# Identities multiplied into a free bank during two waits of TensorE, and experts copied on chip instead of gathered

## What is computed

```python
h = jnp.square(jax.nn.relu(jnp.einsum('bsd,fd->bsf', x, W_fc)))
y = jnp.einsum('bsf,df->bsd', h, W_proj)
def step(mem, _):
    reset = jax.lax.stop_gradient(spike_fn(mem - THRESHOLD))
    mem_new = BETA * mem + y - reset * THRESHOLD
    spk = spike_fn(mem_new - THRESHOLD)
    return (mem_new, spk)
_, spks = jax.lax.scan(step, mem0, None, length=NUM_STEPS)
return jnp.sum(spks, axis=0) / NUM_STEPS
```

```python
ffn_probs = jax.nn.softmax(jnp.mean(n2, axis=1) @ ffn_rw + ffn_rb, axis=-1)
topk_p, topk_i = jax.lax.top_k(ffn_probs, K)
topk_p = topk_p / jnp.sum(topk_p, axis=-1, keepdims=True)
sw1 = fw1[topk_i]
sw2 = fw2[topk_i]
h = jax.nn.gelu(jnp.einsum('btd,bkdf->bktf', n2, sw1), approximate=False)
eo = jnp.einsum('bktf,bkfd->bktd', h, sw2)
return x + jnp.einsum('bktd,bk->btd', eo, topk_p)
```

## Time and profile before

| what | value |
| --- | --- |
| runs | 2107.44, 2114.57, 2112.74 us; median 2112.74 |
| profiled execution | 2107.44 us, span 2105.7 us |
| TensorE busy | 1726.3 us, 82% of the span |
| VectorE busy | 1291.6 us, 61% |
| ScalarE busy | 1169.0 us, 56% |
| GpSimd busy | 611.3 us, 29% |
| mean granted clock of TensorE | 0.904 of full speed |

### The profile page before, as it was taken

How to read it: one execution, slowest core, us unless ns; L and a number is a source line. 1 busy time by engine, 2 the same in 40 slices (tenths; PEclk the granted TensorE clock), 3 DMA queues, 4 the chain that set the end, 5 groups by cost and what they waited for, 6 DMA issues and landing times.

```text
span 2105.7 us, 36738 instructions
## 1 busy us (share of the span) xinstructions
PE 1726.3 (82%) x13696; PEld 902.9 (43%) x13696; DVE 1291.6 (61%) x2587; ACT 1169.0 (56%) x2722; POOL 611.3 (29%) x759
## 2 busy tenths in 40 slices
PE   5997889798898979889588885968999676899976
PEld 1555345533355425543244332323554352355435
DVE  4775478545776467745477267636878445678844
ACT  3565355543465536565256554554888635388862
POOL 2552155300544035410255103313332031333202
PEclk9999999999899989999679696986999988699997
DMA  4000000000000000000252000005443020544303
GB/s 174 17 17 7 0 16 17 12 0 1 16 12 17 1 11 17 17 1 0 45 99 50 1 1 0 0 18 110 89 97 74 2 80 8 111 97 94 76 2 100
DMA packets 55272, 79.21 MB, mean 38 GB/s; under 512 B 6004, under 2 KB 38996, under 8 KB 54584
## 3 DMA queue, kind: packets, MB, share of 16 engines
q1 hardware_dynamic: 52536, 68.47, 14.8%
q0 software_dynamic: 2560, 8.39, 1.3%
HBM read 50.59 MB, written 16.88 MB: 32 GB/s over the span
## 4 chain that ended last, share of the span: by engine, by line
PE 58%; DVE 16%; ACT 13%; issue 7%; DMA 3%; POOL 3%; SPq 0%; DVEq 0%; POOLq 0%; ACTq 0%
PE ps L195 53%; ACT arena L583 4%; DVE arena L1331 2%; PE ps L476 2%; ACT arena L1310 2%; DVE arena L654 2%; ACT arena L260 1%; ACT arena L262 1%; DVE arena L697 1%; DVE arena L1078 1%; DMA arena<-scratch 1%; DMA arena<-arena 1%; PE ps L1226 1%; PE ps L568 1%; DVE arena L1340 1%
## 5 line engine op out<-in xcount | busy, mean ns | idle before, releaser
L195 PE MATMUL ps<-arena 32*64 32x128 f32 (+10 forms) x10192 | 720.8, 317 | 123.6 <-ACT arena L1310 27.5
L195 PEld LDWEIGHTS ps<-arena 128*18 128x18 f32 (+6 forms) x10192 | 409.0, 127 | 430.1 <-issue 118.9
L1331 DVE TENSOR_REDUCE arena<-ps 128x2 f32<-128x512 f32 x512 | 322.4, 685 | 108.9 <-PE ps L195 106.9
L1310 ACT ACTIVATE arena<-ps 128x512 f32<-128x512 f32 (+1 forms) x640 | 333.8, 575 | 78.8 <-PE ps L195 70.2
L195 PE MATMUL ps<-arena,w_L0f 128*128 128x512 f32 (+3 forms) x800 | 340.0, 555 | 36.1 <-ACT arena L303 14.5
L583 ACT ACTIVATE arena<-ps,arena 128x128 f32<-128x128 f32 x512 | 226.5, 460 | 132.1 <-DVE arena L699 132.1
L195 PE MATMUL ps<-arena,const 128*128 128x512 f32 (+1 forms) x528 | 187.5, 652 | 48.5 <-DVE arena L1759 21.8
L195 PEld LDWEIGHTS ps<-arena,w_L0f 128*128 128x128 f32 (+2 forms) x800 | 143.0, 195 | 170.8 <-issue 126.5
L779 POOL TENSOR_TENSOR arena<-arena 128x512 f32<-128x512 f32 x128 | 133.0, 1046 | 238.2 <-DVE arena L671 238.2
L654 DVE TENSOR_TENSOR arena<-ps,arena 128x1024 f32<-128x1024 f32 x128 | 153.2, 1205 | 22.9 <-PE ps L195 22.9
L594 ACT ACTIVATE arena<-ps 128x512 f32<-128x512 f32 x128 | 76.8, 600 | 127.5 <-DVE arena L654 124.7
(11 more groups left out here) (227 smaller groups left out, 2178.2 us busy)
## 6 DMA issues: line engine op xcount, KB each, us to landing
scratch<-arena SPq DMA_DIRECT2D x40, 384.0 KB, 2.8
arena<-scratch SPq DMA_DIRECT2D x80, 192.0 KB
arena<-scratch SPq DMA_DIRECT2D x80, 128.0 KB
arena<-arena SPq DMA_DIRECT2D x64, 128.0 KB, 2.3
arena<-scratch SPq DMA_DIRECT2D x80, 88.0 KB
w_L0f<-in_L0f SPq DMA_DIRECT2D x2, 1557.0 KB, 12.1
arena<-arena SPq DMA_DIRECT2D x80, 12.0 KB
const<-in_const SPq DMA_DIRECT2D x1, 1276.0 KB, 7.4
```

What stands on the lines that cost most here:

```text
L195: return self.nc.tensor.matmul(o, lhsT, rhs, start=start, stop=stop, skip_group_check=True)
L1310: S.activation(self.pt[g % 4][:, e, 0:both], ps[:, self.shifted_bank(2 * g + e), 0:both], ACT.Exp, scale=self.scale).then_inc(self.exped.s ...
L1331: o = V.tensor_reduce(mx, ps[:, self.score_bank(s), :].rearrange("p (t s) -> p t s", t=2), AXX, ALU.max)
```

## The change

Three edits.

First, a new method `warm(bank, n)` issues `n` matmuls of the identity with 512 columns of the mask table, bfloat16, into a bank whose content nobody reads afterwards. It is called in the sum of the last chunk of a Spike stage, four matmuls ahead of each of the five counts, into bank 0 once the last Relu has read it, and in L3Experts once behind the router's matmuls, 24 matmuls.

Second, L3Experts loads all eight experts into the `arena` at the start of the stage, by eight plain DMAs of 256 KB that SyncE issues. GpSimd has no work in the stage any more.

Third, VectorE copies each slot's expert from there to `chosen[n]`: it loads the slot's column number (now the expert's number times 512) from the SBUF into a register and copies 128x512 from that column on. It picks three slots ahead of its loop and then one per turn, ahead of the gate. TensorE waits for `picked` instead of the DMA.

```diff
+    def warm(self, bank, n):
+        for _ in range(n):
+            self.mm(self.ps[:, bank, :], self.ident_b[:], self.masks_b[:, 0:BANK])
...
         for i in range(SPIKE_STEPS):
+            if c == NCHUNK - 1:
+                self.wait_ge(eng, self.relued, 4 * NCHUNK)
+                k.warm(0, 4)
             self.wait_ge(eng, self.spiked, SPIKE_STEPS * c + i + 1)
...
+AHEAD = 3
...
+        self.experts = a.take(EXPERTS * EXPERT_N)
...
         self.router.tensor(eng)
+        k.warm(0, 24)
...
-                eng.wait_ge(self.arrived[n].sem, self.arrived[n].at(16))
+                self.wait_ge(eng, self.picked, n + 1)
...
-        ch.did(V.tensor_scalar(self.rowf, self.rowf, k.C("partition"), None, ALU.add))
+        ch.did(V.tensor_scalar(self.rowf, self.rowf, float(EXPERT_N // P), None, ALU.mult))
         ch.wait_ge()
         V.tensor_copy(self.row_no, self.rowf).then_inc(self.rows_ready.sem, 1)
+        self.wait_ge(eng, self.arrived, 16 * EXPERTS)
+        self.wait_ge(eng, self.rows_ready, 1)
+        for n in range(AHEAD):
+            self.pick_expert(eng, n)
         for n in range(N + 2):
+            if n + AHEAD < N:
+                self.pick_expert(eng, n + AHEAD)
...
-    def gpsimd(self, eng, ch):
-        G = self.k.nc.gpsimd
-        self.wait_ge(eng, self.rows_ready, 1)
-        for n in range(TOP_K * BATCH):
-            b, x = n // TOP_K, n % TOP_K
-            rows = self.row_no[:, x * BATCH + b:x * BATCH + b + 1]
-            eng.indirect_dma_start(self.chosen[n], None, self.k.ins["experts"], bass.IndirectOffsetOnAxis(ap=rows, axis=0)).then_inc(self.arrived[n].sem, 16)
+    def pick_expert(self, eng, n):
+        i = n % TOP_K * BATCH + n // TOP_K
+        at = eng.value_load(self.row_no[0:1, i:i + 1], min_val=0, max_val=(EXPERTS - 1) * EXPERT_N)
+        self.k.nc.vector.tensor_copy(self.chosen[n], self.experts[:, bass.ds(at, EXPERT_N)]).then_inc(self.picked.sem, 1)
+
+    def sync(self, eng):
+        for e in range(EXPERTS):
+            eng.dma_start(self.experts[:, e * EXPERT_N:(e + 1) * EXPERT_N], self.k.ins["experts"][e * P:(e + 1) * P]).then_inc(self.arrived.sem, 16)
```

More of the change, by code:

```diff
@@ L2019, in __init__ @@
         self.added = self.sig("added", BATCH)
-        self.arrived = [k.flag(f"expert_arrived{n}", 16) for n in range(N)]
+        self.arrived, self.picked = self.sig("arrived", 16 * EXPERTS), self.sig("picked", N)
     def tensor(self, eng, ch):
```

## The result

| | runs | median | lowest to highest |
| --- | --- | --- | --- |
| before | 4 | 2110.88 us | 2107.44 to 2114.57 |
| changed | 4 | 2083.47 us | 2073.53 to 2089.41 |

The account below looks back on a forecast made before the run. Stages run one after another, bound by VectorE in Spike's last firings, TensorE in the norm and expert loop. Gains 6.1 + 2.2 + 2.4 = 10.7 us off 2107.44, plus 5.3, gave 2102.0 us; range 2095 to 2111.

Parts of the forecast that it names:

- part 1: Experts stage: replacing gathers by plain loads and VectorE picks shortens TensorE's first wait, 6.1 us gained over both runs.
- the 1.6 forecast: Experts stage: first expert matmul 1.6 us after the order, from 1.1 load, 0.35 copy and 0.15 semaphore.
- their 5.3 us: Whole kernel: the profiled execution lay 5.3 us under the runs' median, so 5.3 was added to the sum.
- The register load and VectorE's queue: Experts stage, VectorE: load with register work 1.1 us, copy 0.35; in the loop taken as hidden, costing nothing.
- the 0.15 for the semaphore: Experts stage: signal from the first copy to TensorE's first expert matmul, 0.15 us.
- The 2.3 us taken as a ceiling: Experts stage: upper limit for the register load, taken as the quickest DMA landing between two SBUF places.
- The stall of 0.7 to 0.9 us: Experts stage: at the high clock TensorE waits 0.7 to 0.9 us per stage for the first gate.
- The rivals that let VectorE set the pace: Experts loop: picks bind TensorE, about 2110 us, chance 0.12; VectorE in a row or load 2.3, 2119, 0.10.
- The 24 identities: Experts stage, behind the router: identities save cold work at the start of the expert matmuls, 2.2 us.
- The Spike identities: Last five counts of both Spike stages: keeping the clock up into the next norm, 2.4 us of 0 to 5.5.
- The range: Whole kernel: 2095 to 2111 us, leaving out the slowest case and about a tenth of the rest.
- small chance of a slowdown: Whole kernel: slower than before with chance 0.10, the case at 2119 us.

Follow-up runs that it names:

- e2: The kernel before with only the loads at the stage's start and the picks on VectorE, no identities: 2089.0 us, ratio 0.9963.
- e9: The kernel before run against itself, nothing changed: 2107.5 us, ratio 0.9992.
- e12: The kernel before with only the identities ahead of the last five counts in both Spike stages: 2103.9 us, ratio 0.9973.
- e6: The changed kernel without the 24 identities behind the router: 2085.1 us, ratio 0.9879 to the kernel before.
- e3: The kernel before with only the 24 identities behind the router, gathers kept: 2101.1 us, ratio 1.0012.
- e16: The changed kernel with identities in attention, 24 between norm and router and 36 behind the router: 2086.6 us, ratio 0.9936 to the kernel before.
- e15: The changed kernel with 32 and 12 more identities in each of three attention stages: 2092.6 us, ratio 0.9968 to the kernel before.
- e5: The changed kernel as it is, run again: 2081.8 us, ratio 0.9869 to the kernel before.
- e7: The changed kernel with 36 identities instead of 24 behind the router: 2081.5 us, ratio 0.9867 to the kernel before.
- e8: The changed kernel with 36 identities behind the router and 24 between norm and router: 2080.4 us, ratio 0.9862 to the kernel before.

## Why the prediction was wrong

**The step that failed** is the price of the gathers, in part 1. "So TensorE waits 4.82 and 4.46 us behind the order, for a gather that lands 4.03 us after its issue": I took this as all that the gathers cost, and the picks' gain as this wait less the new one, 6.1 us. The wait was read rightly, and so was what replaces it (1.33 and 1.60 us against the 1.6 forecast; e2's loops 6.6 us shorter). But behind it, while the other gathers run, TensorE's signals to ScalarE and VectorE can be late, by up to 6.7 us. The one trace that I had showed no such delay, and no other was there to show it. On chip C it costs 2.9 to 7.2 us per stage run (loops of 38.9 to 43.2 instead of 36.0), on average 8.8 us per launch over e9 and e12, and there the picks gain 19.0. For the first result itself this is argued: its traced execution of before has no late signal, and its other three were not traced.

That the trace and the runs were at odds could have been seen: it took 2107.44 us at a clock of 0.904, which is about what an undelayed execution takes at such a clock (chip A: 2101.4 to 2107.5 at 0.905 and 0.906), but the two other runs, 2112.74 and 2114.57, needed either a still lower clock or another cause. I added their 5.3 us to the end as a constant, on both sides of the change, and did not ask whether the change would take them away.

**The register load and VectorE's queue** were right in kind, too dear in size. A pick takes 0.75 us with its copy, 0.32 of it idle, against 1.1 and 0.35; from the cast's end to the first copy it is 0.84 and 1.12 us. That the first matmul came at the forecast 1.6 us and better is in part luck: the load and its register work took less than 1.1, the copy 0.43 instead of 0.35, and the 0.15 for the semaphore, for which the prediction had no row, was 0.06. (The 2.3 us taken as a ceiling is a median of 64 DMAs, not their quickest.) The Trainium skill's page "DMA: Bandwidth & Descriptors" (section on latency and other measured facts) puts the floor of such a load at some 600 ns; the 0.84 us, with three register instructions in it, agree. The stall of 0.7 to 0.9 us for four picks ahead of the first gate did not come: the loop's matmuls start without a gap. The rivals that let VectorE set the pace are refuted by GELUs 1.73 us apart.

**The 24 identities**, 2.2 us, were worth 1.5 to 3.1 by the loops of e6 and the four traces of the changed kernel, and nothing alone (e3), as the reasoning on idle gaps had it: the clock falls again behind 2.55 us of waiting in the first result. The gain is that it comes back after 3.4 us.

**The Spike identities**, 2.4 us, are the second term that was mis-sized: they were worth 5.3 in the profiled pair and 4.0 and 5.9 by the runs. Here the term was halved for the case that the clock falls in the 1.2 us around the last count. It held through the first tail in every trace with these identities, and through the second in all but two (e12 and e16, low for 3.4 us, some 1.5 us lost). The rows had spoken for it: "1.53 held, 2.26 fell", and the idle stretches here are 0.5 and 0.85 us. The middle between 0 and 5.5 was caution without a row.

**The sum.** The touched stages gave 13.3 us, the parts on chip A 10.9, the forecast 10.7. Up to there the working holds, but that 10.9 meets 10.7 is luck: on chip A the picks gave 9.5 for 6.1, the 24 identities -2.6 for 2.2, the Spike identities 4.0 for 2.4. Of the rest up to 24 to 30 us, about 9 are the signals; the remaining few us lie, as far as the one profiled pair shows, in the clock of stages that the change does not touch. Their share is about the width of the intervals, and whether they come by chance or from the change's moving of the stages is open.

**The range** was too narrow in any case. It took in the unknown prices, but not that one kernel's runs lie 20 us apart on one chip and its means up to 13 us between chips. Direction and the small chance of a slowdown were right.

## What to carry to other kernels

Price a stream of indirect gathers by more than its landings: ask who exchanges signals while it runs, and look for engines that start several waiting steps at once as the stream ends. Small tables that can be read whole are loaded ahead by plain DMAs and picked on chip, for 0.75 us each. Filling a wait of TensorE pays where the filling reaches close to the real work and displaces nothing (Spike, 0.85 us ahead of the norm, 4 to 6 us for 40 matmuls), not where a longer wait follows it (e3) or the filling itself takes TensorE's time (e15). And before a small effect is read from one pair of traces, compare the clock of the stages that did not change.

## What was not expected of the hardware

- Signals from TensorE to ScalarE and VectorE were up to 6.7 us late while GpSimd's gathers ran, on two chips of four, and in the loop three of them came together as the gathers ended (1706.00, 1706.12, 1706.24). The same kernel takes 2098.6 and 2098.9 us on the other two, 2109.8 to 2111.9 on these.
- The clock held over 0.85 us of idleness behind a stretch in which TensorE stood idle 0.54 us ahead of each count, one every 1.79 us. Ahead of the first expert it held behind 1.03, 1.13, 2.33 and 2.39 us and fell behind 2.55, 2.61, 2.82 and 3.06 (changed kernel, e5, e7, e8). In e15 44 matmuls of filling did not keep it up in attention, where 14.5 of 16 busy us ran at 0.50.
- A copy of 128x512 at a column number from a register takes 0.43 us, hardly more than the 0.35 that half of the earlier trace rows gives for a fixed one.
